# The keys of a batch in another order: runs of eleven in the copy of turned keys, and values read back in eight transfers

## What is computed

```python
x = x + einsum('bct,bcd->bdt', x, w0[cond])            # a matrix picked for each batch mixes its tokens
q, k, v = project(x)                                   # 8 query heads, 4 key/value groups of 32 columns
q, k = rope(rms(q), pos), rope(rms(k), pos)            # pos = kv_len + token
k_blocks[blk, :, off, :] = k; v_blocks[...] = v        # new keys and values written into a pool of blocks of 16 keys
scores = einsum('bghtd,bgsd->bghts', q, k_all) / 16    # all keys of the batch's block table (257 blocks)
allowed = (kpos <= pos) & (kpos > pos - 128)           # a window of 128 positions
x = x + (softmax(where(allowed, scores, -inf)) @ v_all) @ Wo.T
x = x + einsum('bct,bcd->bdt', x, w2[subj])            # again a matrix for each batch
x = x + (x @ W.T + low-rank adapter picked by batch)
```

## Time and profile before

| | us |
|---|---|
| span of the profiled execution, first to last instruction | 556.0 |
| timed executions of the kernel | 558.14 (median), 560.75, 554.74 |
| PE busy in the span | 466.1 (84%) |
| DVE busy | 413.0 (74%) |
| ACT busy | 341.7 (61%) |
| POOL busy | 205.6 (37%) |
| DMA, mean over the span | 162 GB/s |

### The profile page before, as it was taken

One profiled execution on the slowest core, in us unless ns is written; L12 is line 12 of the kernel. 1 busy time (PEld: TensorE's weight loads), 2 busy tenths in 40 slices (PEclk: granted clock), 3 DMA queues, 4 the chain that ended last, 5 costly groups with the idle time before them and its releaser, 6 DMA issues.

```text
span 556.0 us, 15369 instructions
## 1 busy us (share of the span) xinstructions
PE 466.1 (84%) x4726; PEld 386.1 (69%) x4726; DVE 413.0 (74%) x1357; ACT 341.7 (61%) x1075; POOL 205.6 (37%) x236
## 2 busy tenths in 40 slices
PE   0648899980015999999999999999999999999996
PEld 0537799970014688778778877877887887888884
DVE  7965577954116888888888878888888888788651
ACT  6238454455004677677777777768677775877662
POOL 7422588979603132332314324152331423211000
PEclk9999999995557899999999999999999999999999
DMA  7977776658266575757667596875858769645000
GB/s 231 293 271 306 242 219 203 201 176 199 67 155 144 146 179 150 171 142 182 155 132 179 129 174 159 151 175 124 181 139 134 182 144 182 153 127 128 13 21 19
DMA packets 97784, 90.09 MB, mean 162 GB/s; under 512 B 22967, under 2 KB 93655, under 8 KB 94972
## 3 DMA queue, kind: packets, MB, share of 16 engines
q1 hardware_dynamic: 82384, 52.58, 38.6%
q0 software_dynamic: 9312, 31.58, 22.1%
q10 hardware_dynamic: 6056, 5.54, 3.0%
HBM read 78.02 MB, written 35.65 MB: 204 GB/s over the span
## 4 chain that ended last, share of the span: by engine, by line
issue 47%; PE 12%; POOL 10%; DMA 3%; POOLq 1%; ACT 1%; DVE 0%; ACTq 0%; DVEq 0%
POOL old L862 4%; PE bank L1328 3%; DMA new<-written_blocks,g_idx 3%; POOL new L871 3%; POOL rms L828 3%; PE bank L1339 2%; PE bank L1354 2%; PE bank L1311 1%; POOL g_idx L855 1%; PE bank L1292 1%; PE bank L1306 1%; PE bank L1312 1%; PE bank L1329 1%; PE bank L1300 1%; PE bank L1287 0%
## 5 line engine op out<-in xcount | busy, mean ns | idle before, releaser
L828 POOL TENSOR_TENSOR rms<-rms,halfpow 128x8 f32<-128x8 f32 x48 | 86.1, 1793 | 247.4 <-DVE rms L576 247.4
L1130 ACT ACTIVATE p_room<-bank,nmax 128x176 f32<-128x176 f32 x256 | 101.4, 403 | 79.0 <-DVE nmax L704 74.9
L1328 PE MATMUL bank<-blocks_room,qbd 128*128 128x176 f32 x512 | 127.1, 352 | 6.6 <-issue 5.5
L1328 PEld LDWEIGHTS bank<-blocks_room,qbd 128*128 128x128 f32 x512 | 78.5, 193 | 26.6 <-issue 7.8
L1339 PE MATMUL bank<-ident,p_room 128*88 128x128 f32 x512 | 77.9, 275 | 4.8 <-DVE p_room L749 4.2
L704 DVE TENSOR_REDUCE nmax<-bank 128x2 f32<-128x352 f32 x128 | 66.6, 521 | 20.4 <-PE bank L1329 17.6
L1143 ACT ACTIVATE pT_room<-bank 88x512 f32<-88x512 f32 x128 | 75.1, 587 | 0.4 <-PE bank L1339 0.4
L749 DVE TENSOR_SCALAR p_room<-p_room,rrec 128x176 f32<-128x176 f32 x256 | 70.1, 316 | 5.6
L1339 PEld LDWEIGHTS bank<-ident,p_room 128*88 128x88 f32 x512 | 57.5, 123 | 15.9 <-DVE p_room L749 8.7
L712 DVE COPY blocks_room<-bank 128x352 f32<-128x352 f32 x64 | 47.5, 747 | 22.2 <-PE bank L1287 22.2
L1329 PE MATMUL bank<-pen,mask_sel 128*128 128x176 bf16 x256 | 61.9, 242 | 0.0
(11 more groups left out here) (199 smaller groups left out, 938.4 us busy)
## 6 DMA issues: line engine op xcount, KB each, us to landing
values_by_group<-new SPq DMA_DIRECT2D x16, 704.0 KB
blocks_room<-values_by_group SPq DMA_DIRECT2D x8, 704.0 KB
v_room<-values_by_group SPq DMA_DIRECT2D x8, 704.0 KB
xin<-in_x_dram SPq DMA_DIRECT2D x32, 128.0 KB
x_spill<-v_room SPq DMA_DIRECT2D x32, 128.0 KB
q_spill<-v_room SPq DMA_DIRECT2D x32, 128.0 KB
written_blocks<-new ACTq DMA_DIRECT2D x2, 2048.0 KB, 8.7
blocks_room<-q_spill SPq DMA_DIRECT2D x32, 128.0 KB
```

The costliest lines, as they stand in the source:

```text
L828: pool.tensor_tensor(out=rms[:, i, 2, :], in0=rms[:, i, 1, :], in1=halfpow[:, :], op=ALU.pow).then_inc(s_rstd, 1)
L1130: last = a.activation(pex[k % 2][:, h, :], ps_s[k % 2][:, h * KEYS:(h + 1) * KEYS], ACT.Exp, bias=nmax[:, k % 4, h:h + 1], accum_out=rsum[ ...
L1328: mm(dst, qbd[grp % 2][:, f, h, :], kT[grp % 2][:, f, :, :].rearrange("p w o -> p (w o)"), start=True, stop=False)
```

## The change

The 176 keys of a batch stand in the order (c, o, w) in place of (w, o'): key 16w + 2o + c, with c the parity of the offset in the block (2), o half of it (8) and w the block (11). Five places follow:

- `kT` is laid out (batch, c, o, w); the copy after a turning step writes runs of w, 11 adjacent floats.
- A step turns four offsets of the same parity: k0 and k2 the even ones, k1 and k3 the odd ones.
- `keypos` gets its numbers in the new order from the one iota.
- A row of `vg`, p = 11o + w, now holds keys 16w + 2o and 16w + 2o + 1 as its two halves, which are adjacent in `values_by_group`. The readback becomes eight transfers (HB = 8), one per o, of 11 partitions x 8 batches x 1 KB, in place of one of 88 partitions x 16 runs of 512 bytes.
- `s_vin` counts 128 per group in place of 16.

```diff
-        turned = room[:, 0:2 * BLOCK * ROWS].rearrange("p (i f w o) -> p i f w o", i=2, o=BLOCK, w=W)
+        turned = room[:, 0:2 * BLOCK * ROWS].rearrange("p (i f c o w) -> p i f c o w", i=2, f=GB, c=2, w=W)
...
-                        o = 4 * int(kind[1])
-                        v.tensor_copy(kT[n % 2][:, :, :, o:o + 4].rearrange("p f w o -> p o f w"),
+                        c, o = int(kind[1]) % 2, 4 * (int(kind[1]) // 2)
+                        v.tensor_copy(kT[n % 2][:, :, c, o:o + 4, :].rearrange("p f o w -> p o f w"),
                                       ps_m[bank][:, 0:4 * ROWS].rearrange("p (o f w) -> p o f w", o=4, w=W)).then_inc(s_empty[bank], 1)
...
-            make(pool.iota(key_i[:, :], pattern=[[1, KEYS]], base=0, channel_multiplier=0))
+            make(pool.iota(key_i[:, :], pattern=[[1, 2], [2, HB], [BLOCK, W]], base=0, channel_multiplier=0))
...
-                        sp.dma_start(vg[i][:, :, :, :].rearrange("p f c d -> p (f c) d"),
-                                     v_d[2 * it + grp, :, :].rearrange("(a p) d -> p a d", p=HK)).then_inc(s_vin[i], 16)
+                        by_key = v_d[2 * it + grp, :, :].rearrange("(f w o c) d -> o w f (c d)", f=GB, w=W, c=2)
+                        for o in range(HB):
+                            sp.dma_start(vg[i][W * o:W * o + W, :, :, :].rearrange("p f c d -> p f (c d)"), by_key[o]).then_inc(s_vin[i], 16)
...
-                    i, o0 = n % 2, 4 * int(kind[1])
+                    i, odd, o0 = n % 2, int(kind[1]) % 2, 4 * (int(kind[1]) // 2)
...
-                        last = turn_over(m[:, ROWS * o:ROWS * o + ROWS], new[i][0:ROWS, o0 + o, 0, :], ident[0:ROWS, 0:ROWS])
+                        last = turn_over(m[:, ROWS * o:ROWS * o + ROWS], new[i][0:ROWS, 2 * (o0 + o) + odd, 0, :], ident[0:ROWS, 0:ROWS])
...
-                        mm(dst, qbd[grp % 2][:, f, h, :], kT[grp % 2][:, f, :, :].rearrange("p w o -> p (w o)"), start=True, stop=False)
+                        mm(dst, qbd[grp % 2][:, f, h, :], kT[grp % 2][:, f, :, :, :].rearrange("p c o w -> p (c o w)"), start=True, stop=False)
...
-                        pe.wait_ge(s_vin[kb // GB % 2], 16 * (it + kb // 16) + 16)
+                        pe.wait_ge(s_vin[kb // GB % 2], 16 * HB * (it + kb // 16) + 16 * HB)
```

## The result

The changed kernel takes 552.46 us (median of 20 runs, 547.58 to 555.0), the kernel before 556.68 us (20 runs, 550.82 to 560.75); the ratio is 0.9922, 95% interval 0.9897 to 0.9948. The change brings 0.8%, some 4 us; forecast was no difference, 557.8 us. The profiled execution has a span of 545.8 us against 556.0; at 547.58 us it is the fastest of the twenty, so the two profiles differ by more than the kernels do. In all that follows medians are over all runs of a kernel, and each ratio leaves out, on both sides, the runs over 1.5% above the fastest of their kernel (none of these forty, three of six in the last experiment). Lines behind line 998 have moved by one.

What follows compares the result with a forecast made beforehand. PE's own instructions were taken to bound 320 of the 556 us; -0.4 (first copies) - 0.6 (first values) + 0.7 (refill, late store) = -0.3 us, so 555.7, or 557.8 us on the median's scale; range 552.5 to 562.5.

Steps and rivals of the forecast that it cites:

- The copy's duration: Copy of turned keys on DVE: 747 to 540 ns, bounds 518 (149 + 352 x 1.05) and 747; saves 13.2 us busy time.
- In the 320 us of the steady part that is nothing: From 200 to 520 us the shorter copy gains no time, since PE's own instructions are the limit.
- PE's waits name DVE nowhere there: Steady part: PE waits 5.3 us for its own issue and 0.3 for a gather, never for DVE; held against DVE's relief counting.
- Rival 1: DVE's relief counts in full, a busy PE hiding stalls in modelled ends: up to 14.7 us, 543.4, half 550.8; chance 0.11.
- the half price: Half of DVE's relief comes back as time: 550.8 us; the 0.11 chance covers whole or half.
- full price: All of DVE's relief comes back as time: up to 14.7 us, 543.4 us on the median's scale.
- The start: Start of the slots: -0.4 us first copies, -0.6 first values, +0.7 refill and late store, in sum -0.3 us.
- The issue: Eight readback issues on SP take 4.6 us, the last 4.0 us after the first (bounds 2.3 and 13.7).
- the landing: First readback's last part lands 2.1 to 4.3 us after its issue, at 177.8 to 180.0; taken 178.9, 0.6 us won.
- The late store and the refill: Group 1's store, issued later behind the readback, and the refill needing it near 191 us: 0.7 us lost, bounds 0 and 3.
- Packets: Hardware queue: 82,384 to about 71,100 packets; 470 us of engine time saved or, at twice the cost, nothing; half taken.
- Rivals 2 and 3: First readback late at the start, 566 to 568 us; or every readback late in the steady part, near 628; together 0.07.

Runs made afterwards that it cites:

- the last experiment: Kernel before, VectorE's order untouched, with TensorE's waits for the mask and the masked product moved to the products that read them: 551.8 us, ratio 0.9858.
- the copy alone: Changed kernel with values read back in one transfer, keeping the new key order and new copy (values paired with wrong keys): 551.59 us, ratio 0.989.
- the second profiles: Both kernels run once more without edits: the changed one 553.13 us, ratio 0.991; the one before 556.52 us, ratio 0.9993.

## Why the prediction was wrong

**The copy's duration.** Forecast 540 ns with a floor of 518; measured 514. The floor from the slope of two other instructions, 149 + 352 x 1.05, was the right value, and odd starts cost nothing that shows: half of the runs of eleven begin on an odd float, and the group stands at 514 ns. The Trainium skill, page Vector Engine (DVE) Microarchitecture Reference, section 5.2, has its slower rate, 1.30 ns, for pairs that start on an odd word on both sources; the prediction's estimate of 560 ns took it over to runs of eleven at a destination, and for these it doesn't hold. The lower of its figures for single words at a destination, 1.71 ns for hops of 4 KiB, is met by the 1.70 of before with its steps of 64 bytes.

**"In the 320 us of the steady part that is nothing. PE's work hides it."** This step failed. Three readings led to it. The busy share of 97.6% was taken as PE's own work, though a matmul is drawn to its modelled end: when the next one comes 0.25 us late, the record before covers most of it. The waits labelled "issue" were taken as PE's own; five were (the turn of the loop), six were the mask. And the waits were read for PE alone: PEld's named line 738 with 6.0 us and 20 waits. "PE's waits name DVE nowhere there" was true of the view that I had read, and wrong of the engine. The forecast asked how much work an engine has; the question was which instruction of VectorE PE waits for, and what is queued ahead of it. Of a group's eight slots one has a copy (k2) ahead of the mask and two have one (k0, k3) ahead of the masked product. In place of the nothing that the sum had for the steady part, the runs showed 0.66 us a loop of 16 batches at the mask and 0.43 at the last products, an estimated 9 us in the two first profiles and some 4 us, net of the start, by the medians.

**Rival 1, the relief of DVE counts.** It had the mechanism (modelled ends that hide stalls) and the half price, 550.8 us; measured were 552.46. I gave it a chance of 0.11, on the strength of the earlier trace rows. Its full price was too high by a third: the duration fell by 0.233 us a copy, the queue by 0.17, so 10.9 us and not 14.7. By the medians the copy alone brought 5.8 us, about half of that; by the loops of single profiles it brought 2.2 us and the change 9.2 and, by the second profiles, 8.3. By the order of the code a copy with no deadline behind it (k1) gives nothing directly, which no run tried. Once PE comes sooner the gathered keys are late instead; how often they are differs from execution to execution.

**The start.** Forecast -0.3 us in sum; the eight transfers cost 1.8 us there. The issue took less than thought (4.6 forecast; 3.1 in the start, 4.0 in the steady part at 407.77). The first of the eight goes out 7.85 us behind the first keys (167.63 less 159.78), the one transfer went out 7.94 behind them (171.74 less 163.80). But the first sum of values came 17.0 us behind the keys, where the forecast had 178.9 - 163.8 = 15.1. The term that failed is the landing: from the last issue at about 170.7 to the sum at 176.8 are 6 us, where I had taken 2.1 to 4.3. One large transfer with the same bytes needed 7.8 us from issue to use; splitting it didn't shorten that. The query load behind stood 10.8 us in the queue (3.97 before) and no wait of PE was put down to it. It is not a fixed time behind the last issue that was wrong, but the packets' own time, which the term left out: they were under way until 175.48, at 108 ns each.

**The late store and the refill.** Forecast a loss of 0.7 us; VectorE waited 0.24 us for it at 188.53, and in the copy alone, without the eight issues, 0.87. So that term exists, is small, and doesn't need the eight transfers.

**Packets.** Forecast 71,100; measured 72,352. Their share of the engines' time rose from 38.6 to 40.1% of a shorter span: 0.386 x 556.0 = 214.6 us and 0.401 x 545.8 = 218.9 us of each engine. The packets missing from the count are there with another size: 1,232 more of 4 bytes, 11 for each of the 112 additional transfers. And no relief is seen from runs of 1 KB: over the whole span the 22,528 packets of 512 bytes that went had taken 1021 us, 45 ns each, and the 11,264 of 1 KB that came took 1054 us, 94 ns each. Of the two bounds "twice the time for twice the size" was the right one.

**Rivals 2 and 3.** The first readback came 1.8 us later, not 8 to 10, and in the steady part no wait of PE for values showed. The fixed costs of eight transfers didn't come one behind another.

## What to carry to other kernels

When an engine is busy in 97% of a stretch, measure the distance between the starts of its instructions at the same place of each round, and read the waits of the weight loads too, before you call the stretch bound by its work. Then ask of each small instruction that the engine waits for what is queued ahead of it; moving a 0.75 us copy behind two such deadlines gave as much here (0.9877) as making it 0.23 us shorter did (0.9922), without a new order of data and without seven more transfers a group. The intervals of these two overlap, so which of them is faster is not shown.

A copy that writes single floats 64 bytes apart pays an estimated 1.70 ns an element, and runs of eleven pay 1.04 (747 and 514 less the 149 of the prediction's slope, over 352). That is worth having, but a change of layout that buys it has to be charged for what it does to the transfers on the other side, 1.8 us here.

## What the runs showed of the hardware

Runs of eleven floats, half of them at odd places, are written from PSUM at the rate of contiguous ones: 514 ns for 352 elements against 518 by the slope of two contiguous operations, and 521 for a maximum over as many. Instructions of VectorE overlap at their ends: a copy of 747 ns holds up the next for 0.60 us, one of 514 for 0.43, and what a chain gains is the difference of these. A late mask comes and goes with the same instructions: with the copy alone it was late by some 0.5 us at batch 4 of four loops in a row and then no more, and by 0.45 us at batch 12 of every second loop, and in the changed kernel's second profile in the first loop only; what switches it is open. Packets of 1 KB took 94 ns where two of 512 bytes took 90, and 108 where two took 78 in the start. And two executions of one kernel can bring the first keys 2.8 us apart (163.80 and 160.97 before), which is a good part of the spread of the runs.
